# One decoder layer on one core: four pieces of a hand-written order of work moved

## The reference

```python
# x: (4, 1024, 1024); w_qkv: (1024, 3072); w_out: (1024, 1024); 16 heads of 64
qkv = layernorm(x) @ w_qkv
q, k, v = heads_of(qkv);  q = q / sqrt(64)
scores = where(causal, q @ k.T, -1e10)          # (4, 16, 1024, 1024)
x = x + (softmax(scores) @ v) @ w_out
# then: x += xattn(layernorm(x), ctx_1024)      # 512-wide context, 128-wide queries and keys
#       x += ffn(layernorm(x))                  # choice of one of 8 experts, rank 8
```

## Time and profile before

| | before |
|---|---|
| time, median of 3 runs | 2594.27 us (2590.72 to 2594.79) |
| time of the profiled execution | 2594.27 us |
| its span | 2592.5 us |
| PE busy | 2384.6 us, 92% of the span |
| DVE busy | 1800.0 us, 69% |
| ACT, POOL busy | 822.7 us, 714.2 us |
| mean granted TensorE clock | 0.973 |

### The profile page before, as it was taken

One profiled execution on the slowest core, in us unless ns is written; L12 is line 12 of the kernel. 1 busy time (PEld: TensorE's weight loads), 2 busy tenths in 40 slices (PEclk: granted clock), 3 DMA queues, 4 the chain that ended last, 5 costly groups with the idle time before them and its releaser, 6 DMA issues.

```text
span 2592.5 us, 38046 instructions
## 1 busy us (share of the span) xinstructions
PE 2384.6 (92%) x14411; PEld 1165.3 (45%) x14411; DVE 1800.0 (69%) x3457; ACT 822.7 (32%) x1629; POOL 714.2 (28%) x981
## 2 busy tenths in 40 slices
PE   4888989799999999899999999989999999998997
PEld 1334444454544444454454444445444444445444
DVE  6667788656967777756876776765695767675567
ACT  2444343312223343421213333341122433342110
POOL 3322444224312222213412222222431222221221
PEclk9999999899999999999999999989999999999997
DMA  7688888866647767866746677786674687686643
GB/s 217 160 175 188 205 182 183 204 148 149 139 107 146 153 141 153 186 152 149 158 114 138 138 147 145 152 195 151 148 144 103 138 160 137 135 187 153 114 74 106
DMA packets 983131, 393.50 MB, mean 152 GB/s; under 512 B 936796, under 2 KB 946012, under 8 KB 982948
## 3 DMA queue, kind: packets, MB, share of 16 engines
q1 hardware_dynamic: 980356, 381.63, 68.3%
q10 hardware_dynamic: 2592, 9.44, 1.2%
HBM read 122.56 MB, written 33.55 MB: 60 GB/s over the span
## 4 chain that ended last, share of the span: by engine, by line
PE 68%; DVE 19%; DMA 4%; issue 4%; ACT 3%; POOL 2%; SPq 0%; ACTq 0%; DVEq 0%; POOLq 0%
PE ps_p L570 10%; PE ps_p L571 10%; PE ps_p L572 10%; PE ps_o L657 8%; PE ps_s L630 7%; PE ps_s L570 6%; PE ps_s L572 6%; PE ps_s L571 6%; DMA r<-pn 3%; DVE peak L932 3%; DVE pn L892 2%; DVE bn L897 2%; PE ps_s L635 2%; ACT probs L809 2%; DVE vn L1167 2%
## 5 line engine op out<-in xcount | busy, mean ns | idle before, releaser
L1188 POOL TENSOR_SCALAR pn<-probs,rden 128x640 f16<-128x640 f32 (+7 forms) x512 | 396.9, 788 | 1231.0 <-DVE rden L944 699.0
L809 ACT ACTIVATE probs<-ps_s,low,sizes 128x640 f32<-128x640 f32 (+7 forms) x512 | 421.7, 827 | 770.1 <-DVE low L935 652.2
L892 DVE SCALAR_TENSOR_TENSOR pn<-probs,rden,pn 128x640 f16<-128x640 f32 (+7 forms) x512 | 442.9, 902 | 137.0 <-POOL pn L1188 135.4
L570 PE MATMUL ps_p<-r,w 128*128 128x512 f16 x1344 | 515.0, 383 | 6.1 <-DVE qk L892 6.0
L571 PE MATMUL ps_p<-r,w 128*128 128x512 f16 x1344 | 514.7, 383 | 0.0
L572 PE MATMUL ps_p<-r,w 128*128 128x512 f16 x1344 | 513.7, 382 | 0.0
L630 PE MATMUL ps_s<-qk 64*128 64x512 f16 (+3 forms) x2304 | 241.9, 336 | 92.3 <-ACT probs L809 85.9
L932 DVE TENSOR_REDUCE peak<-ps_s 128x2 f32<-128x1280 f32 (+3 forms) x128 | 241.5, 1887 | 94.0 <-PE ps_s L635 93.7
L657 PE MATMUL ps_o<-r,vn 128*64 128x512 f16 (+3 forms) x2304 | 214.6, 343 | 32.9 <-issue 32.5
L572 PEld LDWEIGHTS ps_p<-r,w 128*128 128x128 f16 x1344 | 132.6, 99 | 162.1 <-issue 6.3
L570 PE MATMUL ps_s<-r,pn 128*128 128x512 f16 x512 | 195.0, 381 | 9.4 <-DMA pn<-pn 9.4
(11 more groups left out here) (191 smaller groups left out, 3441.4 us busy)
## 6 DMA issues: line engine op xcount, KB each, us to landing
w<-w_pairs SPq DMA_DIRECT2D x72, 512.0 KB, 4.0
r<-wo_pairs SPq DMA_DIRECT2D x16, 1024.0 KB, 6.4
w_raw<-in_x SPq DMA_DIRECT2D x32, 512.0 KB, 4.2
out<-r SPq DMA_DIRECT2D x32, 512.0 KB, 2.9
w_pairs<-w SPq DMA_DIRECT2D x24, 512.0 KB, 4.8
qk<-in_x SPq DMA_DIRECT2D x24, 512.0 KB, 4.5
w_raw<-in_ctx_t SPq DMA_DIRECT2D x16, 512.0 KB, 4.7
w_raw<-in_w_qkv ACTq DMA_DIRECT2D x12, 512.0 KB, 5.1
```

The costliest lines, as they stand in the source:

```text
L570: pe.matmul(ps, lh, rh, start=start and k == ks[0], stop=False)
L809: act.activation(probs_part(q, j, w), ps_s[:, j, scores(q)], ACT.Exp, bias=low[:, n % 2, i:i + 1], scale=sc(n), accum_out=den[:, n % 2, i: ...
L892: dve.scalar_tensor_tensor(out=to, in0=bank, scalar=scale, in1=rounded, op0=ALU.mult, op1=ALU.subtract).then_inc(ok, 1)
L1188: pool.tensor_scalar(to, src, scale, 1.0, ALU.mult, ALU.mult).then_inc(ok, 1)
```

## The change

Four things are moved.

1. PE: `P212+` comes ahead of `S0+ S1+`, in all 28 bodies.
2. DVE: `L60 L61` come ahead of `X7`, in all 28 bodies; `WL0++` comes ahead of `CL11+` and `WL1++` ahead of `R7` (pairs 2 to 7 of batch 0).
3. SP, batch 0: the stores `WS0`, `WS1` of pair n + 2 are issued behind `T6` of unit n, not behind `T0` and `T1` of unit n + 1, and `WS2+` behind `T1`, not `T2`; those of pair 1 go into the start. `SI05` is loaded behind `T6` of unit 0, not `T0` of unit 1, and `SN04`, `SN05`, `SN10`, `SN11` on ACT come one block earlier (behind `E11`, `E21`).
4. SP, p = 6 of each batch: `JI0`, `JI1`, `KI` are issued together behind `T6`, not behind `T3`, `T4`, `T5`. `KI` now waits for all projections of the last pair (up to `P213+`), and `KH` and `KL` have no such wait of their own.

```diff
 PE_BODY = """
...
-    P111+ P112+ P113+ S7 P200+ P201+ P202+ P203+ P210+ P211+ S0+ S1+ P212+ P213+
+    P111+ P112+ P113+ S7 P200+ P201+ P202+ P203+ P210+ P211+ P212+ S0+ S1+ P213+
 DVE_BODY = """
...
-    X5 L40 L41 R5 CL10+ X6 OL0 WC++ L50 L51 R6 CL11+ X7 WL0++ L60 L61 R7 WL1++ CL20+
+    X5 L40 L41 R5 CL10+ X6 OL0 WC++ L50 L51 R6 WL0++ CL11+ L60 L61 X7 WL1++ R7 CL20+
 SP_BODY = """
-    WD2+ T0 WS0+ T1 WS1+ T2 WS2+ T3 T4 WD0++ T5 T6 WD1++ T7 V+
+    WD2+ T0 T1 WS2+ T2 T3 T4 WD0++ T5 T6 WS0++ WS1++ WD1++ T7 V+
 SP_START = """
...
-    WI2++ WS0+ WS1+ WS2+ V+
+    WI2++ WS0+ WS1+ WS2+ WS0++ WS1++ V+
...
-for pair, at, row in ((0, "T0", (0, 1, 2)), (0, "T4", (3,)), (0, "T5", (4,)), (1, "T0", (5,)),
+for pair, at, row in ((0, "T0", (0, 1, 2)), (0, "T4", (3,)), (0, "T5", (4,)), (0, "T6", (5,)),
...
-        (n, "E41"), (n, "E51"), (n, "E61"), (n, "E71"), (n + 1, "E21"), (n + 1, "E31"))]):
+        (n, "E41"), (n, "E51"), (n, "E61"), (n, "E71"), (n + 1, "E11"), (n + 1, "E21"))]):
...
-    ONCE["SP", pair, "T3"] = "JI0"
-    ONCE["SP", pair, "T4"] = " ".join([ONCE.get(("SP", pair, "T4"), ""), "JI1"])
-    ONCE["SP", pair, "T5"] = " ".join([ONCE.get(("SP", pair, "T5"), ""), "KI"])
+    ONCE["SP", pair, "T6"] = "JI0 JI1 KI"
...
                     elif kind == "KI":
-                        sp.wait_ge(part_ok, 6 * PAIRS * (b + 1) - 4)
+                        sp.wait_ge(part_ok, 6 * PAIRS * (b + 1))
...
                     elif kind == "KH":
                         act.wait_ge(k_in, 16 * (b + 1))
-                        act.wait_ge(part_ok, 6 * PAIRS * (b + 1) - 2)
...
                     elif kind == "KL":
                         dve.wait_ge(kh_ok, b + 1)
-                        dve.wait_ge(part_ok, 6 * PAIRS * (b + 1))
```

## The result

| | before | after |
|---|---|---|
| time, median of 4 runs of each, side by side | 2594.47 us | 2613.43 us |
| ratio, 95% interval | | 1.0083 (1.0069 to 1.0095) |
| profiled execution, span | 2592.5 us | 2613.8 us |
| PE busy, DVE busy | 2384.6, 1800.0 us | 2387.5, 1819.5 us |

What follows compares the result with a forecast made beforehand. PE was taken as the bound, nearly gapless in batches 1 to 3, with open time in batch 0. Bodies +10.8, tails +9.6, batch 0 -7 gave +13.4 on 2594.27 us, rounded to +12: 2606 us (2600 to 2611; wide 2592 to 2620).

Steps and rivals of the forecast that it cites:

- The seam of batches 1 to 3: Bodies following a body: T7 issued later, S4 waits, 0.6 us each, 18 x 0.6 = +10.8 us (2 to 18).
- The tails: Four tails behind bodies: M1 waits 2.4 us longer for T7's landing, 4 x 2.4 = +9.6 us (5 to 15).
- The term for KI: Tails: KI's 512 KB in flight when T7 starts, T7 lands later, +1.1 us (0 to 2.5).
- The term for L71: Tails: T7's later issue behind L71 is added in full to M1's wait, 1.4 us.
- Batch 0: Batch 0's bodies: gains of 13 us at waits and clock, losses of 6, together -7 us (-22 to +6).
- S0 waits for E71 by 1 to 2 us: Batch 0, 6 seams: X7 some 3.4 us later, S0 waits 1 to 2 us, S2 0.7 to 2 longer; +6.
- less 2 for the idle time that is now split and lets the clock stay up: Batch 0 seams: split idle time keeps the clock up, taking 2 us off the +6 loss.
- +2 for T7: Batch 0: T7 meets WS0, WS1 and two WI loads, 1 to 4 us later in four units; +2 remain.
- (a): T7's delay is hidden, S4's slack covers the rest, bodies cost 0.1 us; 2593 us; chance 0.19 with its surroundings.
- (b): Batch 0's exposed waits go altogether, 24 us gained without loss at the seams; chance 0.09.
- (c): DVE and POOL hinder each other in full: X7 +2.9, `low` +0.4 at 21 seams; 2613 us; chance 0.14.
- (d): JI0, JI1, KI and in batch 0 the stores delay T7 by 2 us and more each time; 2620 us; chance 0.13.

Runs made afterwards that it cites:

- P212 alone: Kernel before with only P212 moved ahead of S0 on PE; ratio 1.0038, 2601.07 us against 2589.76.
- the rests alone: Kernel before with only L60 and L61 moved ahead of X7 on DVE, WL0 staying behind X7; ratio 1.0109, 2620.76 us.
- the loads alone: Kernel before with only JI0, JI1, KI issued behind T6, KI waiting for all of the batch's pieces; ratio 1.0040.
- the stores alone: Kernel before with all of part 3 (WS stores, SI05 and SN moves), PE and DVE as before; ratio 1.0031.
- the chain alone: Kernel before with SI05 behind T6 of unit 0 and SN04, SN05, SN10, SN11 one step earlier, stores unmoved; ratio 0.9996.
- the change without the loads: Changed kernel with JI0, JI1 and KI at T3, T4 and T5 again; ratio 1.0100 against the kernel before.

## Why the prediction came out as it did

**The seam of batches 1 to 3: right.** X7 was to be 2.6 us later and is 2.65; S2 +0.1, measured 0.13; T7's issue at 1.4 us behind S2, measured 1.33; S4's wait 0.5 to 0.6, measured 0.55; a body 47.1, measured 47.2 to 47.3. The sum of +10.8 came out as +10.0, of which unit 29 gave back 3.3 by chance. The closeness of the sum is luck in part: the 17 other bodies that follow a body cost 12.3 us, 0.72 each and not 0.6. What the prediction did not ask is which edit costs this. Either is enough: P212 alone makes S0 late by a piece, the rests alone make H71 late, for which `low` waits.

**The tails: the sum right, its terms not.** 2.4 us a tail were forecast, as a longer wait of M1. The tails are 2.0 us longer each, and so much later behind S2 does M1 start, but its own wait grew by only 1.15; some of the rest is S3 ahead of it, whose wait in the tail of batch 1 went from 3.03 to 3.50 us. The term for KI was taken at 1.1 us from the earlier trace rows; by themselves the three loads measure 2.4, of which 0.5 are the queue. The term for L71 was taken at 1.4, and P212 alone lengthens the four tails by 5.1 us. Together they would have been 15 and are 8.1: in the change T7 starts 1.32 us behind S2 with the loads or without them, so the queue costs nothing, as the prediction had it. KI is issued 1.3 us ahead of T7 in place of 0.45, JI0 and JI1 5.8 in place of 2.9, and T7 holds the queue for 5.48 us in the tail of batch 1 and not 6.80.

**Batch 0: the step that failed.** The prediction had "-13 + 6 = -7"; measured is +3.0. The time was missed by 7.4 us. In the account of the trace this step alone is 10.0 us off, more than the chance of a stretch, and the other two parts together 2.3 the other way, so part of the closeness is luck. Two terms of the losses were mis-sized. First, "S0 waits for E71 by 1 to 2 us" and S2 0.7 to 2 us longer, +6 in all. S0's wait is 3.17 us, six times. The prediction had X7 later by 3.4 us, and counted from P211 it is later by 5.3, since H60 waits for WL0, and L60 for H60. S0's and S2's waits in these six seams rose from 11.3 to 22.2 us, and at the seam behind unit 6, which the prediction didn't count, S2 waits 1.87 us where it had no wait: together +12.7, not +6. Second, "less 2 for the idle time that is now split and lets the clock stay up": the piece behind S0's wait runs at the granted clock of 0.50 and lasts 2.8 us, and PE's busy time rose by 0.8 us. All other waits of PE in these bodies together fell by 10.3 us; that and some small gaps make idle time +2.2, and with the 0.8 the bodies are 3.0 longer. So the gains came nearly as forecast (-13, and +2 for T7): S5 5.71 to 0, M1 of unit 2 7.13 to 0, P110 of units 3 to 5 6.0 to 0.6; against them stand 3.34 and 1.90 us at M1 and M0 of unit 1, 2.63 at S4 of unit 2 and 1.52 at P110 of unit 6.

**The rivals.** (a), T7 hidden: out, by S4's wait in every body. (b), batch 0 gains 24 us: out; S0's and S2's waits eat the gains, and the stores ahead of T7, alone, cost more than they free. (c) gave 2613 and the time is 2613.4, but not by its account: `low` costs 0.13 us a seam in the steady bodies and not 0.4. What it was about is real where POOL is full, in batch 0. The Trainium skill (SBUF — State Buffer, section "SBUF: two separate sides") calls the port pair that VectorE and GpSimd share an exclusive lock, held for the whole instruction by whoever starts first. The traces agree, with 1.09 us for `low`, 2.13 for L70 and 2.95 for H60 and H61. What the prediction quoted of it, two inputs in SBUF, fits L70, which reads `probs` and `pn`; `low` reads one tensor, so that clause doesn't account for it, though it too ends with H71. (d), loads and stores delay T7 by 2 us and more: true of the loads alone (2.4) and of the stores alone (M1 of unit 1, 7.8 us more than with the chain alone). In the change as a whole it is true of unit 1 alone in batch 0 (M1 waits 3.34 us); in the tails M1 waits 1.15 us longer in the mean.

## What to carry to other kernels

Before a step is moved ahead of another, ask for both what the next transfer waits for, and measure its slack: here 0.66 us of slack at S4 decided 18 bodies, and two edits that use up the same slack cost it once. Costs of edits that end in the same wait don't add up, neither when put in nor when taken back, so an edit whose removal gains nothing isn't free. In these traces a big transfer issued ahead of one that is waited for cost more at a distance of 0.5 to 2 us than at 1.3 to 5; putting the stores where the queue was idle gained 0.22%. And where one stretch of one trace varies by 5 us with the same code, its difference shows little: the length of a single wait at a named step is the firmer reading.

## What was not expected of the hardware

How long the transposed copy T7 holds its queue varies at the same place: ahead of unit 2 it is 11.24 us when two stores of 512 KB were issued 2 us before it, 5.51 when they were issued 5.4 us before, but also 10.38 in the kernel before and 5.44 with P212 alone, with no store ahead. In the steady seam it is 4.85 us. What part the other loads have in it (two that ACT issued 6 to 7.5 us ahead of T7 with the stores alone and in the change) wasn't tried by itself. And an instruction of two elements a partition can cost 1.09 us on VectorE if GpSimd has one of 1024 running: the price depends on the neighbour and not on its own size.

What stays open: why the change without the loads is not faster, though M1 waits less in its tails; and how much of batch 0's account is chance of the transfers, since M1 of unit 2, 7.13 us in the trace of before, was 5.01 us in the kernel with the loads alone, which is the same up to there.
